# Perceiver layer with a selective-scan mixer on one core: the skip term of the scan moved from VectorE to TensorE and ScalarE, with a new order of the middle stages

## The reference, cut to what matters

```python
u = jax.nn.silu(conv(x @ in_w.T + in_b))             # 512 inner channels
delta = jax.nn.softplus(delta_lr @ dt_w.T + dt_b)
deltaA = jnp.exp(einsum('bld,dn->bldn', delta, A))   # 16 states
deltaBu = einsum('bld,bln->bldn', delta * u, Bm)
carry = dA * carry + dBu;  ys = carry.sum(-1)        # scan over the 32 tokens
y = ys + u * D_param                                 # the skip term
out = y @ out_w.T + out_b
```

## Time and profile before

| what | value |
|---|---|
| median of three runs | 1050.1 us (1049.0 to 1051.41) |
| the profiled execution | 1048.12 us, its span on the core 1046.3 us |
| busy TensorE / VectorE / GpSimd / ScalarE | 937.7 / 894.2 / 857.6 / 755.5 us |
| phase 0 with the preparation | 79.3 us |
| phase 1 (no "post" yet) | 116.4 us |
| phases 2 to 7, each | 116.5 us |
| phase 8 (no "pre") | 102.6 us |
| phase 9 (feed-forward alone) | 49.1 us |
| table loads on ScalarE in a steady phase | 8 (4 before exp, 2 silu, 2 softplus) |

### The profile page before, as it was taken

The page is one execution under the profiler, slowest core; times in us unless marked ns, Lnnn a source line. Parts: engine busy times, 40 slices in busy tenths (PEclk is TensorE's granted clock), DMA queues, the critical chain, the costliest instruction groups (busy, mean ns, idle before and its releaser), DMA issues.

```text
span 1046.3 us, 13080 instructions
## 1 busy us (share of the span) xinstructions
PE 937.7 (90%) x4175; PEld 508.2 (49%) x4210; DVE 894.2 (85%) x1210; ACT 755.5 (72%) x1319; POOL 857.6 (82%) x617
## 2 busy tenths in 40 slices
PE   9886988999989998999899998999899999677986
PEld 6553443546445554546345454545354554432554
DVE  1433988899989999899989999899989999899945
ACT  2346658877797869877897869876987869765634
POOL 1368999899979898899979898898989897999800
PEclk9998998999999999999999999999999999899999
DMA  9903620445043610544042610454042301300000
GB/s 353 357 1 162 234 109 1 162 136 208 0 144 113 230 41 2 182 162 182 1 177 86 223 40 20 163 185 158 2 182 81 122 1 55 128 0 1 1 20 21
DMA packets 21916, 116.33 MB, mean 111 GB/s; under 512 B 3480, under 2 KB 4120, under 8 KB 9305
## 3 DMA queue, kind: packets, MB, share of 16 engines
q1 hardware_dynamic: 16232, 80.70, 20.9%
q10 hardware_dynamic: 5616, 34.81, 9.1%
HBM read 111.04 MB, written 4.46 MB: 110 GB/s over the span
## 4 chain that ended last, share of the span: by engine, by line
PE 29%; DVE 24%; ACT 19%; POOL 16%; issue 10%; DMA 1%; ACTq 0%; DVEq 0%; POOLq 0%
PE bank L1253 13%; DVE state L1119 13%; PE acc L1253 11%; POOL state L827 11%; ACT decay L898 6%; DVE raw L1099 3%; POOL state L835 2%; ACT u L991 2%; ACT u L999 2%; ACT L898 2%; ACT soft L882 2%; DVE sg L1169 1%; PE decay L1253 1%; DVE hm L1182 1%; POOL rstd L785 1%
## 5 line engine op out<-in xcount | busy, mean ns | idle before, releaser
L1119 DVE TENSOR_TENSOR_SCAN state<-decay,state 128x512 f32<-128x512 f32 (+1 forms) x352 | 590.3, 1696 | 42.9 <-ACT decay L898 28.9
L827 POOL TENSOR_TENSOR state<-w,brep 128x512 f32<-128x512 f32 (+1 forms) x352 | 612.1, 1768 | 0.2
L1253 PE MATMUL acc<-state,ident 128*128 128x512 f32 x832 | 406.5, 605 | 18.4 <-DVE state L1119 14.0
L898 ACT ACTIVATE decay<-delta,neg_a 128x496 f32<-128x496 f32 x512 | 329.4, 669 | 86.6 <-DVE state L1119 85.2
L1253 PEld LDWEIGHTS acc<-state,ident 128*128 128x128 f32 x832 | 148.1, 191 | 165.9 <-issue 116.3
L835 POOL TENSOR_TENSOR state<-state 128x512 f32<-128x512 f32 x96 | 122.0, 1271 | 43.9 <-DVE state L1119 42.6
L882 ACT ACTIVATE soft<-x_in,nmr,rstd 128x256 f32<-128x256 f32 x64 | 33.2, 589 | 52.5 <-POOL nmr L788 52.5
L1253 PE MATMUL bank<-xn_t,in_w 128*128 128x512 f32 x128 | 61.1, 611 | 5.8 <-DVE u L1245 4.3
L1253 PE MATMUL bank<-out_w,u 128*128 128x256 f32 x256 | 58.0, 382 | 6.7 <-DVE u L1108 6.7
L926 ACT ACTIVATE sg<-bank,ag 128x512 f32<-128x512 f32 x64 | 43.6, 681 | 26.4 <-PE bank L1253 25.6
L860 POOL TENSOR_TENSOR w<-delta,u 128x512 f32<-128x512 f32 x32 | 39.9, 1266 | 26.3 <-ACT delta L1026 26.3
(11 more groups left out here) (147 smaller groups left out, 1312.0 us busy)
## 6 DMA issues: line engine op xcount, KB each, us to landing
keys<-in_keys_t SPq DMA_DIRECT2D x32, 1028.0 KB, 5.9
brep<-b_scratch ACTq DMA_DIRECT2D x32, 1024.0 KB, 7.2
keys<-in_keys_n SPq DMA_DIRECT2D x29, 1024.0 KB
out<-x_in SPq DMA_DIRECT2D x16, 256.0 KB, 5.9
x_in<-in_x SPq DMA_DIRECT2D x14, 256.0 KB
u<-in_keys_n SPq DMA_DIRECT2D x1, 1024.0 KB
w<-in_keys_n SPq DMA_DIRECT2D x1, 1024.0 KB
delta<-in_keys_n SPq DMA_DIRECT2D x1, 1024.0 KB
```

The lines of the kernel that those rows point to most:

```text
L827: nc.gpsimd.tensor_tensor(state[g % CPT][:, 0:count * tok].rearrange("p (c t) -> p c t", c=count), w[:, m, 0:tok].unsqueeze(1).to_broadcas ...
L898: last = nc.scalar.activation(decay[:, q:q + groups * GSEQ, 1:LEN], d, ACT.Exp, scale=neg_a[:, m, n + i:n + i + 1])
L1119: nc.vector.tensor_tensor_scan(flat, by, flat, 0.0, ALU.mult, ALU.add).then_inc(scan_done, 1)
L1253: return nc.tensor.matmul(o, l, r, start=first, stop=last)
```

## The change

**The skip term.** Before the first block, ScalarE builds four diagonal matrices, `skip[:, m, :] = ident * D[m]`. TensorE adds the product of `skip[m]` and `u[m]` to `acc`, right behind the first products of each tile. What VectorE did in one instruction for each tile is now a plain copy from `acc` to `u` on ScalarE, placed behind the decays of the tile's third slot (`Y_AT = 2`); ScalarE leads by one slot, so the copy is issued at the step of the second slot. `y_last` on ScalarE stands behind the decays of the next block's first slot.

**Room for it.** `z` becomes a view of `x_dbl`, and fourteen small tiles become slices of one, `small`.

**The order.** SECOND, PRE, PRE_END, POST_FIRST, POST and POST_END have new numbers; PREPARE, FIRST, LAST, TAIL and the leads are as they were.

```diff
-Y_AT = 0
+Y_AT = 2
@@ tables: one line of PRE, as it was and as it is
-    ("silu", [61, 67, 67, 67]),
+    ("silu", [67, 67, 67, 67]),
...
+        skip = sb("skip", [P, TILES, P])
...
-        z = sb("z", [P, DIM])
-        x_dbl = sb("x_dbl", [XROWS, TOK])
+        x_dbl = sb("x_dbl", [P, TOK])
+
+        z = x_dbl[:, 0:DIM]
...
@@ scalar
+                def y(block_, odd, m):
+                    n = SIZES[block_] * P
+                    reach(act, summed, block_, (m + 1) * len(SUM_SLOTS))
+                    nc.scalar.activation(u[odd][:, m, 0:n], acc[:, 0:n], ACT.Copy).then_inc(y_ready, 1)
...
+                        if g % CPT == Y_AT and m:
+                            y(b, odd, m - 1)
+                    elif part == "y_last":
+                        y(b, par, TILES - 1)
                     elif part == "mixer_weights":
                         act.wait_ge(w_loaded, 16 * 8)
+
+                        act.wait_ge(a_loaded, 16 * 2)
+                        for m in range(TILES):
+                            nc.scalar.activation(skip[:, m, :], ident[:, :], ACT.Copy, scale=cols[:, D_SKIP, m:m + 1])\
+                                .then_inc(skip_ready, 1)
...
@@ vector
-                def y(block_, odd, m):
-                    n = SIZES[block_] * P
-                    reach(dve, summed, block_, (m + 1) * len(SUM_SLOTS))
-                    nc.vector.scalar_tensor_tensor(u[odd][:, m, 0:n], u[odd][:, m, 0:n], cols[:, D_SKIP, m:m + 1],
-                                                   acc[:, 0:n], ALU.mult, ALU.add).then_inc(y_ready, 1)
...
@@ tensor
+                            if k == 0:
+                                if b == 0 and m == 0:
+                                    pe.wait_ge(skip_ready, TILES)
+                                reach(pe, u_ready, b, m + 1)
+                                mm(acc[:, 0:tok], skip[:, m, :], u[odd][:, m, 0:tok], False, False)
```

More of the change, by code:

```diff
@@ L115 @@
 SECOND = [
-    ("rstd1", [0]),
[L117 to L138, removed]
-    ("stats2", [54]),
[L140 to L155, removed]
+    ("s_neg", [14, 20, 28, 34]),
+    ("p_last", [18, 27, 35, 37]),
+    ("u_evac", [64, 65, 68, 71]),
+    ("exp", [13, 21, 29, 33]),
+    ("stats1", [0]),
+    ("add1", [49]),
+    ("softplus", [83, 87]),
+    ("xn1", [4]),
+    ("b_load", [81, 85, 87, 87]),
+    ("x_proj", [76]),
+    ("turn2", [57]),
+    ("z_evac", [22, 34, 38, 43]),
+    ("attn_out", [46, 46]),
+    ("times_u", [82, 82, 86, 86]),
@@ new lines @@
+    ("zt_evac", [26, 36, 38, 44]),
+    ("mix_in", [62, 62, 63, 67]),
+    ("evac2", [62]),
+    ("query", [7]),
+    ("rstd1", [0]),
+    ("silu", [66, 73, 74, 74]),
+    ("xn2", [57]),
+    ("tap0", [63, 65, 70, 72]),
+    ("evac1", [4]),
+    ("p_turn", [17, 26, 33, 38]),
+    ("q_evac", [10]),
+    ("score", [10, 13, 24, 26]),
+    ("x1", [53, 53]),
+    ("p_sum", [19, 28, 36, 41]),
+    ("s_max", [13, 15, 27, 33]),
+    ("rstd2", [54]),
+    ("attend", [18, 29, 36, 39]),
+    ("add2", [66]),
@@ L168 @@
[L168 to L182, removed]
-    ("z_evac", [22, 30, 34, 43]),
-    ("evac1", [7]),
-    ("z_turn", [23, 28, 34, 43]),
+    ("attend", [18, 23, 30, 39]),
@@ new lines @@
+    ("z_turn", [20, 27, 35, 41]),
+    ("x1", [50, 51]),
+    ("add1", [49]),
+    ("z_evac", [21, 30, 34, 44]),
+    ("rstd2", [52]),
+    ("turn2", [55]),
+    ("turn1", [2]),
+    ("u_evac", [58, 60, 63, 65]),
+    ("evac1", [7]),
+    ("tap0", [60, 61, 66, 66]),
+    ("query", [3]),
+    ("xn1", [3]),
+    ("p_turn", [16, 21, 29, 38]),
+    ("dt", [76, 77, 84, 84]),
+    ("xn2", [54]),
+    ("q_evac", [10]),
+    ("exp", [15, 21, 27, 36]),
+    ("p_sum", [17, 26, 32, 36]),
+    ("s_max", [13, 18, 25, 32]),
@@ L186 @@
+    ("p_evac", [17, 24, 32, 39]),
+    ("zt_evac", [23, 30, 37, 46]),
+    ("add2", [71]),
+    ("x_dbl", [73]),
+    ("softplus", [81, 87]),
+    ("stats1", [2]),
+    ("x_proj", [68]),
+    ("attn_out", [45, 45]),
+    ("times_u", [81, 87, 87, 87]),
+    ("p_last", [15, 21, 29, 37]),
+    ("s_neg", [13, 20, 25, 32]),
+    ("stats2", [52]),
+    ("tap2", [60, 61, 66, 66]),
+    ("score", [5, 16, 22, 28]),
+    ("silu", [67, 67, 67, 67]),
+    ("s_bias", [13, 21, 26, 33]),
     ("mix_in", [57, 58, 62, 62]),
-    ("exp", [13, 20, 28, 38]),
@@ L222 @@
[L222 to L238 removed]
+    ("zt_evac", [25, 32, 39, 46]),
@@ new lines @@
+    ("p_evac", [21, 29, 35, 42]),
+    ("p_last", [19, 25, 32, 40]),
+    ("z_evac", [23, 31, 37, 45]),
+    ("mix_in", [58, 59, 64, 64]),
+    ("dt", [73, 74, 84, 84]),
+    ("s_neg", [14, 19, 28, 38]),
+    ("stats1", [1]),
+    ("turn2", [56]),
+    ("evac2", [58]),
+    ("stats2", [53]),
+    ("silu", [60, 70, 70, 70]),
+    ("softplus", [81, 87]),
+    ("score", [9, 16, 24, 28]),
+    ("times_u", [82, 87, 87, 87]),
+    ("p_sum", [21, 25, 36, 42]),
+    ("add1", [32]),
+    ("add2", [68]),
@@ L239 @@
+    ("rstd1", [0]),
+    ("query", [3]),
+    ("p_turn", [19, 26, 31, 40]),
+    ("s_bias", [15, 22, 29, 38]),
+    ("s_max", [13, 17, 27, 37]),
+    ("attend", [20, 27, 35, 41]),
+    ("tap0", [59, 63, 67, 67]),
+    ("x_proj", [72]),
+    ("turn1", [2]),
+    ("xn1", [3]),
+    ("evac1", [7]),
+    ("z_turn", [22, 30, 38, 43]),
+    ("exp", [16, 24, 29, 39]),
+    ("b_load", [77, 77, 78, 82]),
+    ("attn_out", [46, 46]),
+    ("x_dbl", [75]),
     ("rstd2", [52]),
+    ("tap2", [60, 63, 68, 68]),
@@ L313 @@
+    ("h_max", [21, 29, 52, 72]),
+    ("h_floor", [25, 29, 71, 73]),
 ]
```

209 lines of the change are left out of this document (76 added, 133 removed).

## The result

The changed kernel takes 1062.95 us, the median of four runs (1061.39 to 1066.31), beside 1049.94 us for the kernel before on the same chip: a ratio of 1.0127, 95% interval 1.0099 to 1.0155. It is slower by 13 us. The forecast was 1031 us, with a range of 1011 to 1051 us, and it is wrong in its sign.

What follows compares the result with a forecast made beforehand. Three engines nearly fill the steady phase; the middle of the VectorE and TensorE accounts, 113.8 us, gives -16.2 us over six phases, with the other stretches -18.7, so 1031 us, range 1011 to 1051.

Steps and rivals of the forecast that it cites:

- VectorE account: Steady phase: VectorE loses four y instructions (2.9 us) and 2.3 us of waits, 5.2 us, giving 111.3 us; the good end.
- TensorE account: Steady phase: four skip products add 3.4 us, busy 112.7 us; with 3.6 us idle staying, 116.3 us; the bad end.
- ScalarE's copies: Steady phase: four PSUM to SBUF copies, 2.3 us beside 22 us of slack, hidden behind VectorE's scans.
- block's end: End of a block: of 2.3 us of VectorE waits, 1.3 us stay as gain, with the copy behind the softplus.
- merged silus: Phases 2 to 6: ScalarE loses an extra table load and the return, 1.28 us each, 2.6 us.
- the width: The forecast range, 1011 to 1051 us, meant to cover waits of the new tables, a few us a phase either way.
- slower rival: Steady phase: TensorE keeps 7.2 us idle through later accumulator returns; 119.9 us a phase, launch 1068 us, chance 0.13.
- first to second block: Phase 1: GpSimd's work stays as it was, so only 1 us of gain was given.
- preparation: Before the first block: four 128x128 copies on ScalarE cost 1 to 1.9 us, charged at 1 us.
- eighth phase: Phase 8: three copies replace three steps of 0.73 us, with little TensorE work; 2.5 us gained.

Runs made afterwards that it cites:

- e7b: The kernel before without any y step, copy or product, so the result is incomplete: phase 116.30 us in four of six, launch 1049.03 us, ratio 0.9991.
- e16: e14 with no y step, product or copy, so the result is incomplete: phase 115.68 us, launch 1045.91 us, ratio 0.9952.
- e14: The changed kernel with three entries of POST (rstd3, x2, stats3) as in the kernel before: phase 117.35 us, launch 1053.81 us, ratio 1.0027.
- e13: The changed kernel's order with no y step, product or copy, so the result is incomplete: phases 3 to 6 119.1 us, launch 1063.56 us, ratio 1.0125.
- e11: e7b with times_u changed so GpSimd writes a new block's first inputs earlier: phase 116.4 us in four of six, launch 1048.95 us, ratio 0.9980.
- e8: e1 with the copies on VectorE, where y was, and the product still on TensorE: phase 117.75 us, launch 1059.30 us, ratio 1.0083.
- e9: e1 with only a block's last copy on VectorE, the other three on ScalarE: phase 118.9 us, launch 1069.46 us, ratio 1.0182.
- e10: The kernel before with one order entry changed so the four silus stand together: phase 116.35 us, launch 1049.65 us, ratio 0.9994.
- e1: The skip product on TensorE and copies on ScalarE, with all order tables of the kernel before: phase 119.4 us, launch 1070.74 us, ratio 1.0208.

## Why the prediction was wrong

The steps of one phase now form a chain of measured kernels:

| from | to | phase |
|---|---|---|
| before, 116.48 | `y` and its waits taken out (e7b), 116.30 | -0.2 us |
| e7b | the new order with the norm's entries of before (e16), 115.68 | -0.6 |
| e16 | product and copies added (e14), 117.35 | +1.7 |
| e14 | the three norm entries of the change (after), 119.24 | +1.9 |

All but the last kernel's are phases without a fall of the clock. The split of the last two steps is that of this order of counting: with the norm entries first it is 3.4 and 0.2 (e13).

**The VectorE account failed; the forecast of a gain rested on it.** The prediction took the four `y` steps and the 2.3 us ahead of them as time that the phase would give back: "5.2 us, if nothing else becomes late", 111.3 us. e7b is that case exactly, without TensorE's work or ScalarE's, and gives 0.18 us. The idle time ahead of `y` hid the next release, GpSimd's input, 1.24 us, and the tiles that lost their `y` step gained little: the third stayed at 33.0 us. That other engines are as late there is the reading that fits; e11 shows it for one place only. The forecast was the middle of the two accounts, so half of this error, 2.5 us of the 5.4 by which the phase was missed, went into it. With the account at 0.2 us both accounts would have said 116.3, about no change; that the kernel became slower comes from the terms below.

**The TensorE account was about right in work, wrong in what it adds to.** The product's 3.4 us became 2.6 to 3.0 us of busy time (e14 less e16; e8 less), as allowed for with fewer tails. The 3.6 us of idle that were to stay became 4.9 us in e14 (117.35 - 112.47). Its sum of 116.3 was meant as the bad end and is still 1 us too good for e14.

**ScalarE's copies are not hidden.** The prediction held them for hidden, and left the later return of `acc` to the TensorE account, whose sum has no term for it but half of the old idle time. In the old order they cost 0.8 us a phase alone, and with the product on top 1.7 (119.4 - 117.75). Of the latter 0.5 us is the block's end (e9); by which wait the rest comes was not found.

**The merged silus gave nothing** (e10, 0.1 us a phase). The prediction weighed whether the Trainium skill's 2.66 us for a switch of tables (ScalarE: Activation LUTs, "What ACT_TABLE_LOAD costs") or the trace's 1.28 us holds. The rows of after show 1.28 us again, and e10's ScalarE is busy 2.5 us less, as two loads of 1.28 us make it. But neither figure mattered for the phase; ScalarE was idle 22 us of it already. The merge was tried in the old order only.

**The order was left in the width.** The prediction said that a wait of the new tables "may cost or give a few us a phase", and gave it no row and no chance. It gave 0.6 us and cost 1.9 (or 3.4, counted first), the largest single term of the loss.

**The slower rival came out in size, not in cause.** It gave 119.9 us a phase and 1068 us; measured were 119.2 and 1063. Its mechanism, TensorE keeping its 7.2 us of idle because the accumulator returns later, is shown only for e1 (119.40 - 112.64 = 6.8 us idle). In the changed kernel TensorE is idle 5.3 us, and taking product and copies out altogether leaves the phase as long (e13).

**The ends.** The block's end gained as forecast. The other stretches, in the kernels that take the change apart step by step (one execution each, in us; the clock is at half in parts of most of them):

| stretch | before | e7b | e16 | e14 | after |
|---|---|---|---|---|---|
| start to the first scan | 89.7 | 90.1 | 90.5 | 91.4 | 93.0 |
| first to second block | 106.7 | 105.6 | 103.0 | 101.9 | 101.8 |
| last block's first scan to the end | 151.1 | 149.2 | 151.4 | 153.2 | 153.3 |

The preparation was to lose 1 us and lost 3.3. The four copies that build `skip` are 0.385 us each, 1.3 us together. Single executions scatter here: the eleven kernels that build `skip` reach the first scan at 91.1 to 94.5 us, the eight that don't at 89.7 to 91.9, the medians 2.9 us apart. The first to second block gained 4.9 us where 1 was forecast, the larger part with the new tables (e1, the edit with the old ones, takes 106.1 us). In the last stretch the eighth phase was to gain 2.5 us. Leaving `y` out gives 1.95 there (e7b), so the VectorE account was nearly right for a phase in which TensorE is busy 79 of 102.6 us; the new tables take 2.3 of it back and product and copies 1.8, which makes the loss of 2.2.

Which of the three norm entries does most stays open: they were restored together.

## What to carry to other kernels

Before you count a removed instruction and the wait ahead of it as won, look at what else is ready at that instant on the other engines, and better, build the kernel with the step left out: it prices the best case in one run, and here it was 0.2 us where the rows seemed to offer 5.2. Where several engines are nearly full, as in these phases, work that is moved from one to the next can cost on arrival and return nothing on departure. When an edit comes with a new order, test each with the other held: ten of thirteen lost microseconds were three table entries that had nothing to do with the skip term. And take the parts out in more than one sequence, for two costs can hide each other.
